# GCN sums in sets of 16 and 12 steps, with weighted masks and gathered rows read in place

## The reference

```python
def _conv(x, row, col, edge_type, edge_weight, W, b):
    deg = segment_sum(ones, col, N)
    norm = deg_inv_sqrt[row] * deg_inv_sqrt[col] * edge_weight
    xw = jnp.einsum('ni,tio->tno', x, W)              # 4 edge types
    x_j = xw[edge_type, col] * norm[:, None]          # one row of 128 per edge
    out = segment_sum(x_j, row, N) + b
    return leaky_relu(out, 0.01)
...
x = layernorm(x + (x + z1 + z2 + z3) / 4)
x = layernorm(x + gat(x, ...))
```

## Time and profile before

| what | value |
|---|---|
| median of 3 timed runs | 8944.21 us (8944.13 to 8945.64) |
| the profiled execution, first to last instruction | 11,925.3 us |
| mean granted clock of TensorE, share of full speed | 0.634 |
| POOL busy | 6395.8 us (54%) |
| PE busy | 5307.0 us (45%) |
| DVE busy | 4574.2 us (38%) |
| ACT busy | 3992.0 us (33%) |
| first gather of layer 0 | at 691.5 us |
| last gather of layer 2 | at 8375.1 us |
| attention gathers | 8505.5 to 11,826.8 us |

### The profile page before, as it was taken

The page is one execution under the profiler, slowest core; times in us unless marked ns, Lnnn a source line. Parts: engine busy times, 40 slices in busy tenths (PEclk is TensorE's granted clock), DMA queues, the critical chain, the costliest instruction groups (busy, mean ns, idle before and its releaser), DMA issues.

```text
span 11925.3 us, 149378 instructions
## 1 busy us (share of the span) xinstructions
PE 5307.0 (45%) x32765; PEld 4105.0 (34%) x32766; DVE 4574.2 (38%) x12940; ACT 3992.0 (33%) x12236; POOL 6395.8 (54%) x6521
## 2 busy tenths in 40 slices
PE   5843434434533434343433434343444444444444
PEld 4632322223322323232322323232344444444444
DVE  9952222222322212222322222222555555555556
ACT  6522222222322222222322222222455454445455
POOL 1656566565456565656466565656344444444443
PEclk9975655656655655565655556555566666666666
DMA  1011111111221111111211111111122222222222
GB/s 47 35 42 43 41 44 43 41 44 41 65 55 44 40 44 40 44 40 44 76 42 44 40 44 40 44 40 44 49 69 70 68 71 69 69 68 69 70 69 65
DMA packets 432687, 612.42 MB, mean 51 GB/s; under 512 B 232038, under 2 KB 249491, under 8 KB 432539
## 3 DMA queue, kind: packets, MB, share of 16 engines
q0 software_dynamic: 208832, 428.96, 13.7%
q1 hardware_dynamic: 223707, 182.02, 4.6%
HBM read 437.29 MB, written 51.28 MB: 41 GB/s over the span
## 4 chain that ended last, share of the span: by engine, by line
another core or an unknown queue 48%; DVE 16%; issue 15%; PE 8%; ACTq 5%; DVEq 4%; ACT 3%; POOL 0%; DMA 0%; POOLq 0%; SPq 0%
DVEq L1604 3%; PE bank L1196 3%; ACT g_step L912 3%; ACTq L896 2%; DVE a_miss L1717 2%; PE wide L1196 2%; DVE g_hot L1620 2%; ACTq L912 1%; DVE acc L1634 1%; DVE a_max L1722 1%; DVE lo_hot L1262 1%; DVE acc L1788 1%; PE bank L1191 1%; DVE v_hot L1387 1%
## 5 line engine op out<-in xcount | busy, mean ns | idle before, releaser
L737 POOL DMA_INDIRECT g_rows<-gcn_table,rec_idx x4743 | 4487.1, 946 | 2894.2 <-ACT g_step L912 1484.6
L912 ACT ACTIVATE g_step<-g_rows,rec_w 128x128 f32 x5580 | 1791.5, 390 | 5679.7 <-remote 4618.4
L762 POOL DMA_INDIRECT a_roll<-gat_table,src_plane x1612 | 1524.6, 946 | 1801.0 <-ACT a_cand L937 1375.4
L1634 DVE TENSOR_TENSOR acc<-acc,bank 128x512 f32 x930 | 637.9, 686 | 3828.8 <-remote 3238.9
L1191 PE MATMUL bank<-zeros 1*128 1x512 bf16 x930 | 490.9, 528 | 2909.9 <-DVE acc L1634 2104.6
L1196 PE MATMUL bank<-g_step,g_hot 128*128 128x128 f32 x7440 | 1621.7, 386 | 128.4 <-issue 50.6
L1196 PEld LDWEIGHTS bank<-g_step,g_hot 128*128 128x128 f32 x7440 | 1391.8, 280 | 487.9 <-issue 487.9
L1222 PE MATMUL bank<-a_msg,a_hot 128*128 128x130 f32 x3608 | 798.9, 389 | 1648.7 <-DVE a_msg L1768 1635.0
L1222 PEld LDWEIGHTS bank<-a_msg,a_hot 128*128 128x128 f32 x3608 | 685.6, 283 | 1786.3 <-DVE a_msg L1768 1452.3
L1191 PEld LDWEIGHTS bank<-zeros 1*128 1x128 bf16 x930 | 89.9, 97 | 3099.0 <-DVE acc L1634 2163.3
L937 ACT ACTIVATE a_cand<-a_miss,a_rows 128x128 f32<-128x128 bf16 x3608 | 1095.9, 386 | 14.9 <-DMA a_rows<-a_roll 8.8
(11 more groups left out here) (272 smaller groups left out, 5880.3 us busy)
## 6 DMA issues: line engine op xcount, KB each, us to landing
a_rows<-a_roll SPq DMA_DIRECT2D x451, 264.0 KB
g_rows<-gcn_table,rec_idx POOLq DMA_INDIRECT x4743
gcn_table<-rows SPq DMA_DIRECT2D x147, 256.0 KB
a_roll<-gat_table,src_plane POOLq DMA_INDIRECT x1612
e_dst<-by_dst_dst SPq DMA_DIRECT2D x451, 2.0 KB
gat_table<-acc SPq DMA_DIRECT2D x7, 462.0 KB
out_x<-xs SPq DMA_DIRECT2D x6, 448.0 KB
gcn_slots<-nothing SPq DMA_DIRECT2D x4, 468.0 KB, 6.8
```

The lines of the kernel that those rows point to most:

```text
L737: pool.indirect_dma_start(out=g_rows[:, tile % RING, :], out_offset=None, in_=gcn_tables[layer % 2], in_offset=bass.IndirectOffsetOnAxis(a ...
L762: pool.indirect_dma_start(out=a_roll[:, g % ROLL, t, :], out_offset=None, in_=gat_table, in_offset=bass.IndirectOffsetOnAxis(ap=src_plane[ ...
L912: last = nc.scalar.activation(g_step[:, j, k, :].unsqueeze(1), g_rows[:, bass.ds(slots[k], 1), :], ACT.Copy, scale=rec_w[:, bass.ds(q.at(0 ...
L1634: V.tensor_tensor(dst_ap, dst_ap, sums_of(j).rearrange("p (k d) -> p k d", k=GP), ALU.add).then_inc(s_gadd, 1)
```

## The change

- A set is now four groups (16 steps) or three groups (12 steps) by turns (`SETS`), over seven PSUM banks: the four banks of `wide`, and banks 1 to 3 (`low`). PE clears all banks of a set, does its 16 or 12 step products, closes each bank with a 1-column product, and reports once (`s_gpe`). DVE then adds bank after bank to `acc`.
- ACT's scaling and `g_step` are gone. PE reads the gathered rows in the ring, at slots that it loads itself, and waits for `s_land` itself. POOL waits for `s_gpe` in place of `s_copied`, for whole sets (`reports`).
- The weights go into the masks: for each step one TENSOR_SCALAR of 128x128 compares the numbers 0 to 127, which lie in PSUM bank 0, with the target and multiplies by the weight. `rec_lo` is float32 for this.
- A row of `gcn_at` is four numbers instead of five; the last tile moves to partition 0, column 1, and the attention's slot and block to columns 2 and 3. PE makes three loads per group (tile, slots, places).
- From group 455 on (`ENDING`, 16 groups) single groups are summed as before, with the fill ahead of the loads of the following group. A quarter is padded to 476 steps; 471 groups are summed per layer.

```diff
-RB = 117
+RB = 119
-GRP = Turns(ALL_GROUPS - 3, 9)
+SETS = [4, 3]
+PAIR = sum(SETS)
+SUP = Turns(DONE_FROM // PAIR * 2, 2)
+SUMMED = DONE_FROM // PAIR * PAIR
+ENDING = range(SUMMED - DONE_FROM, NBATCH + 1)
...
-        gcn_at = sb("gcn_at", [65, ALL_GROUPS, GP + 1], I32)
+        gcn_at = sb("gcn_at", [65, ALL_GROUPS, GP], I32)
...
-                            wait_apart(pool, s_copied, layer * GRP.steps - (-steps // GP), s_apart)
+                            wait_apart(pool, s_gpe, layer * POSTS + reports(-(-steps // GP)), s_apart)
...
+                def rows_at(group, steps):
+                    tile = pe.value_load(gcn_at[0:1, group, 1], min_val=0, max_val=CH * CCOLS - 1)
+                    _, slots = nc.values_load_multi_w_load_instructions(
+                        gcn_at[32:33, group, 0:GP].rearrange("p g k -> p (g k)"),
...
+                    _, places = nc.values_load_multi_w_load_instructions(
+                        gcn_at[64:65, group, 0:GP].rearrange("p g k -> p (g k)"),
...
+                def products_of(sums, masks, masked_by, values, closing):
+                    tile, slots, places = values
+                    pe.wait_ge(s_ghot, masked_by)
+                    pe.wait_ge(s_land, tile + (CH * CCOLS * layer + 1))
+                    for k in range(GP):
+                        last = nc.tensor.matmul(sums[:, bass.ds(places[k], D)], g_hot[:, masks, k, :],
+                                                g_rows[:, bass.ds(slots[k], 1), :].rearrange("p o d -> p (o d)"),
+                                                start=False, stop=closing and k == GP - 1)
+                    return last
...
+                def ending(n):
...
+                    fill(sums_of(m))
+                    if n < NBATCH:
+                        ahead.append(rows_at(slice(group + 1, group + 2), GP))
+                    products_of(sums_of(m), m % PAIR, (ADDS - 1) * layer + group + 1, values, True).then_inc(s_gpe, 1)
...
+                def masks(slot, step):
+                    for k in range(GP):
+                        at = bass.ds(step + k, 1)
+                        last = V.tensor_scalar(g_hot[:, slot, k, :], iota_ps, rec_lo[:, at], rec_w[:, at],
+                                               ALU.is_equal, ALU.mult)
+                    last.then_inc(s_ghot, 1)
```

More of the change, by code:

```diff
@@ L99, with first_group, reports @@
 assert len(FOURS) == ROLL
[L100 to L101 removed]
+ENDING = range(SUMMED - DONE_FROM, NBATCH + 1)
+POSTS = SUP.steps + len(ENDING)
+ADDS = DONE_FROM + ENDING.stop + 1
+assert CCOLS == CSPANS * TURN and CSTEPS >= CCOLS + BW + 1 and CSTEPS % (PAIR * GP) == 0
+assert GP * (DONE_FROM + 1) == 3 * CSTEPS + CCOLS + 1 and NB % GP == 1 and ADDS <= ALL_GROUPS + 1
+def first_group(q, lag, plus=0):
+    c = q.base + lag
+    group = PAIR * (c // 2) + (SETS[0] if c % 2 else 0) + plus
+    return group if q.i is None else q.i * PAIR + group
+def reports(groups):
+    pairs, rest = divmod(min(groups, SUMMED), PAIR)
+    return 2 * pairs + (rest > 0) + (rest > SETS[0]) + max(groups - SUMMED, 0)
 class Step:
@@ L539, in body @@
                 if q.live(0):
-                    _, (tile, slot) = nc.values_load_multi_w_load_instructions(
-                        gat_at[0:1, bass.ds(q.at(0), 1), :].rearrange("p g k -> p (g k)"),
-                        engines=(mybir.EngineType.SP,), min_val=0, max_val=GAT_GROUPS - 1,
-                        skip_runtime_bounds_check_because="a step less the begun blocks, at most the last group")
-                    slot = nc.s_assert_within(slot, 0, ROLL - 1,
-                                              skip_runtime_bounds_check_because="a group modulo the ring")
+                    tile = sp.value_load(gat_at[0:1, bass.ds(q.at(0), 1)], min_val=0, max_val=GAT_GROUPS - 1)
+                    slot = sp.value_load(gcn_at[0:1, bass.ds(q.at(0), 1), 2], min_val=0, max_val=ROLL - 1)
                     if q.live(-R):
@@ L1140, in sum_gcn @@
             def sum_gcn(layer):
-                ahead = []
                 def turn(n):
@@ L1165, in body @@
                         return
-                    n = q.base - DONE_FROM if q.i is None else -1
+                    j = q.slot(0)
+                    groups = SETS[j]
+                    values = rows_at(bass.ds(first_group(q, 0), 1), groups * GP)
+                    for k in range(groups):
+                        if q.live(-2):
+                            pe.wait_ge(s_gadd, first_group(q, -2, ADDS * layer + k + 2))
+                        fill(super_sums[j][:, k * GP * D:(k + 1) * GP * D])
@@ new lines, in body @@
+                    for k in range(groups):
+                        now = values
+                        if k + 1 < groups:
+                            values = rows_at(bass.ds(first_group(q, 0, k + 1), 1), groups * GP)
+                        products_of(super_sums[j], SETS[0] * j + k,
+                                    first_group(q, 0, (ADDS - 1) * layer + k + 1), now, False)
+                    for k in range(groups):
+                        last = nc.tensor.matmul(super_sums[j][:, k * GP * D:k * GP * D + 1],
+                                                zeros[0:1, 0:1].to_broadcast([1, P]), zeros[0:1, 0:1],
+                                                start=False, stop=True)
@@ new lines, in ending_masks, with ending @@
+                def ending_masks(m):
+                    group = SUMMED + m
+                    dve.wait_ge(s_gpe, POSTS * layer + reports(group - PAIR + 1))
+                    masks(m % PAIR, group * GP)
+                def ending(n):
+                    group, m = DONE_FROM + n, n - ENDING.start
+                    if m + SETS[0] < len(ENDING):
+                        ending_masks(m + SETS[0])
+                    block, = blocks_of(gcn_at[0:1, group:group + 1, 0], NB - GP)
+                    dve.wait_ge(s_gpe, POSTS * layer + SUP.steps + m + 1)
+                    dst_ap = acc[:, bass.ds(block, GP), 0:D]
+                    dve.wait_ge(s_gadd, adds + 1 + group)
+                    V.tensor_tensor(dst_ap, dst_ap, sums_of(m).rearrange("p (k d) -> p k d", k=GP), ALU.add
+                                    ).then_inc(s_gadd, 1)
+                    if layer == 2 and n >= 1:
+                        masked(n - 1)
+                    if 0 <= n < NBATCH:
+                        dve.wait_ge(s_gadd, adds + 2 + group)
+                        next_z(layer, slice(BATCHES[n].start, BATCHES[n].stop))
+                        if layer < 2:
+                            dve.wait_ge(s_tT, turns(layer + 1, n) + 1)
+                            V.tensor_copy(*turned(n)).then_inc(s_tc, 1)
+                            if n == NBATCH - 1:
+                                chain(V.scalar_tensor_tensor(xs[:, :, :], xs[:, :, :], 1.0 if layer else 5.0,
+                                                             z[:, :, :], ALU.mult, ALU.add))
+                        else:
+                            ln_stats(BATCHES[n], 16.0 * 1e-5)
+                            third(n)
@@ L1652, in layer_gcn @@
+                run_steps(dve, SUP, 1, 1, body)
+                for n in ENDING:
+                    ending(n)
                 dve.wait_ge(s_gadd, adds + ADDS)
```

221 lines of the change are left out of this document (94 added, 127 removed).

## The result

| | median of the runs | profiled execution, first to last instruction |
|---|---|---|
| before | 8944.17 us (4 runs, 8941.71 to 8945.64) | 11,925.3 us (the one read above) |
| changed | 8997.51 us (4 runs, 8994.69 to 9000.4) | 8,993.3 us |
| before, run again (b_again) | 8944.11 us (11 runs) | 8,941.8 us |

The ratio is 1.006, with a 95% interval of 1.0046 to 1.0074: 53 us slower. 8,996 us was forecast. The forecast of the sum was good; two of its terms were not, and they cancelled, as the rows show.

What follows compares the result with a forecast made beforehand. POOL's 6448 gathers, 1.25 us apart (8,060 us), were taken to bound the kernel, almost without pause. Ring filling +10 and ending batches +42 gave +52 us on 8,944: 8,996 us, range 8,900 to 9,080.

Steps and rivals of the forecast that it cites:

- The sum without holes: Whole timed run before the change: start, gathers, tail, ring filling and layer ends sum to 8,990 to 9,024 us without idle holes.
- Terms 1 and 2: ACT's scaling removed and DVE's comparison become four weighted masks; in the layers POOL's 4.3 us a group covers both: 0.
- Term 3: PE's loop: three loads and more register rows need 2.5 us a group, covered by POOL's 4.3 us: 0.
- Term 4: Ring freed by whole sets: the margin of 84 steps stays above 56, so POOL is not held up: 0.
- Term 5: Ring filling in layer 0: 14 groups at 2.5 us instead of 1.75 delay POOL's next gather: +10 us, ends 0 and 20.
- Term 6: Ending batches: three loads between fill and step products cost PE 1.1 us a batch: +42 us, ends 0 and 75.
- Term 7: Shorter memset, six more groups a layer, extra small DVE table operations, the other load on SP: 0.
- Loads hidden: Rival: PE's sequencer runs far enough ahead in the endings, ring no limit in layer 0: 8,944 to 8,960 us; chance 0.22.
- PE becomes the bound: Rival: loads of 1.0 us each make a group 4.5 or 4.6 us, above 4.3: +450, 9,395 us; chance 0.06.
- the lock: Rival: DVE's masks stretch POOL's gathers by 0.1 us on each of 4836: +480, 9,425 us; chance 0.05.
- Faster: Rival: holes partly in timed runs, gathers waiting for ACT's step copies; removing ACT gives back 240 us: 8,700; chance 0.12.

Runs made afterwards that it cites:

- b_again: The kernel before, run again with two more register assertions (one on ACT, one on SP): 8944.11 us, ratio 0.9999.
- experiment 12: Changed kernel with PE's loop loads asked for twice (one more load per group ran), on a chip without holes: 8997.03 us, ratio 1.0062.
- experiments 2 and 3: 2: a_loads_late. 3: kernel before with b_again's assertions and ending loads (two ran) between fill and step products: 8993.82 us, ratio 1.0055.
- a_loads_late: Changed kernel with the ending's three loads moved behind the products, ahead of the transposes: 8964.78 us, ratio 1.0023.
- a_spread_sp_again: Changed kernel; layers 0, 1: loads spread behind table products, masks between z and copy; layer 2: loads behind step products; SP's two loads made one: 8944.34 us, ratio 1.0001.
- a_block_own: Changed kernel with the attention's block numbers in a tile of their own, where the kernel before took 11,930.48 us: ratio 1.0321.

## Why the prediction was right, and where it wasn't

- *The sum without holes.* Right where it mattered: the gathers' four stretches take 8,057.7 us in b_again for 8,060 reckoned, the pauses 29.4, 27.8 and 61.3 for 30, 30 and 70. The tail was taken from the profile with holes at 99 us and is 73.9, and the 10 to 44 us for the ring are 0; these two with the pause ahead of attention are the 0.5 to 0.9% by which the sum was high. Wrong in one sentence: the "idle gathers belong to the profiled execution". They belong to where it ran. Where the kernel before has such holes, 9 timed executions have a median of 11,930 us too. That they weren't in the timed runs of 8,944 us, which the sum made likely, was what counted.
- *Terms 1 and 2 (ACT's scaling, DVE's masks in the loop): 0.* Right. A mask takes 398 ns, but its neighbours overlap it: DVE is busy 1836.1 us with the 1,413 groups' masks, 1.3 us a group for 1.0 to 1.4 reckoned, and gathers stay at 946 ns. In layer 2's ending, with the loads out of the way, a batch takes 7.97 us for 8.13, and the pause is 2.6 us shorter (58.7 for 61.3); whether from ACT's relief or from masks made further ahead wasn't tried.
- *Term 3 (loads in the loop): 0.* Right where POOL is the cover: a layer's gathers last as long as before, and by experiment 12 even with one load more. 2.5 us a group were reckoned, 2.80 measured. One number's load was reckoned at 0.30 us and takes 0.47; four numbers' were reckoned at 0.34 and take 0.33 and 0.50. On the chips with holes the same loads seem not to be covered.
- *Term 4 (the ring freed by sets): 0.* Right: in the changed kernel's loops no gather starts more than 1.4 us behind the one before, once the ring's filling is over.
- *Term 5 (ring filling in layer 0): +10.* Wrong: 0. Its rows came from a stretch with holes. The gathers of layer 0 take 2,017.8 and 2,017.9 us with and without the change. The lower end, 0, had been written down.
- *Term 6 (ending batches): +42, 14 for each layer.* The mechanism is shown by experiments 2 and 3, and the total is 41.6 us. That it comes so near 42 is partly luck, for its split isn't as reckoned: 17.5 and 18.5 us in layers 0 and 1, 5.6 in layer 2. A batch in layers 0 and 1 became 1.6 to 1.8 us longer where 1.1 was reckoned, since a load in the ending takes 0.6 to 0.75 us and not 0.34. Only ten of the twelve steps from batch to batch carry it (the first two take 7.1 and 8.4 us in b_again, 7.2 and 8.7 in the changed kernel). In layer 2 a batch grew by 0.47 us.
- *Term 7 (the rest, "the other load on SP"): 0.* Wrong: +8 to 10 us. The attention's 451 steps, by DVE's a_max, in b_again and in the changed kernel:

```profile
L1724 DVE TENSOR_REDUCE a_max<-wide x451: 1214/1218/1226, 6870.9 to 8886.8; 128x2 f32<-128x1024 f32 x151
```

```profile
L1789 DVE TENSOR_REDUCE a_max<-wide x451: 1214/1218/1226, 6912.5 to 8938.6; 128x2 f32<-128x1024 f32 x151
```

They take 2,015.9 us before and 2,026.1 after, 10.2 more. Between 8,000 and 8,800 us it is 796.4 / 178 = 4.474 us a step before and 795.4 / 176 = 4.519 after, while POOL delivers one every 2,011 / 451 = 4.459. The attention part has hardly any slack, and one load more on SP seems to be enough that the sums fall behind. No run without holes changed that load alone. But all four profiles without holes that have the two loads end 82.4 to 85.1 us behind the last gather, and all three that have one 73.5 to 75.8; and from a_loads_late to a_spread_sp_again, whose other edits lie in the layers' endings, 8.3 us came back. For the other 1.9 us (perhaps DVE's loads from the wider table) the run that would have told fell on the chip with holes.
- *The rivals.* None of them happened. "Loads hidden" is excluded by experiments 2 and 3, "PE becomes the bound" by the loop's 2.80 us a group and gathers that last as long as before, and the lock is real but small where the masks read SBUF. "Faster" rested on POOL's step being nearer 1.0 us; it is 1.25 in each run.

So 8,996 for 8,997.5 owes something to luck: +10 for the ring was not there, +10 behind the last gather was not foreseen.

## What to carry to other kernels

A register load on PE's queue costs only where the array has little work in hand: one of 0.3 to 0.8 us behind each table product of 128x512 cost next to nothing (batches of 5.48 us for 5.28), three in a row between a fill and its product cost 1.6 to 1.8 of their 2.1 us in each batch. A load that is added as a probe and used by nothing may be missing from the program that runs (here the loads of four numbers were, those of one number ran): its count in the trace belongs beside the result. Before durations are read from a trace, its span is set against the timed median; where they differ by a third, single instructions may be used, waits and starting points may not. A chain that keeps pace with its supplier within 1% (here the attention's sums, 4.474 us for 4.459) has no room for even one small load.

## What wasn't expected of the hardware

The same kernel took 8,944 us in three jobs and 11,930 and 12,039 in two others (each job ran on a chip of its own, five chips in all, so it is likely the chip), with single instructions of the same length (gathers 0.95 us, 1.25 apart; batches 5.28 us) and holes of up to 31 us in which ACT, DVE and PE wait for a release that no record shows. The change cost 0.6% on the one and, judged by a_block_own, some 3% on the other, where the pace after a hole seems to count. What makes the holes stays open. A load's length isn't fixed either: the same instruction took 0.33 us in the loop and up to 0.72 in the endings of layers 0 and 1, while in layer 2's ending the three loads took 1.3 us together as in the loop. What lengthens it wasn't tried.
